# A decoder layer on one Trainium2 core: keys and values in one token-major projection, the keys then turned by two transposes

## The chip, the core and the metric

One core of a Trainium2 chip runs the whole kernel. Its engines work side by side, each in its own order, and wait for each other by semaphores: PE (TensorE, matrix products), DVE (VectorE), ACT (ScalarE), POOL (GpSimd) and SP (SyncE, which here only starts DMAs). PE reads SBUF and writes PSUM, which has eight banks of 512 fp32 columns; DVE and ACT read PSUM. The metric is the device time of one execution in microseconds (us), lower is better.

## The reference

A layer of three parts on x of 8 batches x 256 tokens x 512 features, in fp32: a recurrent mixing block with a gated MLP, a cross-attention, and a mixture of experts. The change lies in the cross-attention:

```
q = (Q @ w_q.T).reshape(B, S, G, HG, HD)      # G=8 groups, HG=4 heads each, HD=16
k = (K @ w_k.T).reshape(B, S, G, HD)          # K = V = ctx, 8 x 256 x 512; w_k is 128 x 512
v = (V @ w_v.T).reshape(B, S, G, HD)          # w_v is 128 x 512
scores = jnp.einsum('bnghd,bmgd->bnghm', q, k) / scale
...
attn = jax.nn.softmax(scores, axis=-1)
out = jnp.einsum('bnghm,bmgd->bnghd', attn, v).reshape(B, S, D)
return out @ w_o.T + b_o
```

Scores are masked causally and by a padding mask. The result is added to x, whose rows were normalised before the projection of the queries.

## The kernel before, in words

**Products in three parts.** A projection in fp32 is made of fp32r matmuls: each operand is split into a rounded part (hi) and a rest (lo), and `three` (L780) issues hi x hi, lo x hi, hi x lo into one PSUM region. The first operand is the stationary one (128 columns at most), the second the moving one, streamed column by column.

**Keys, values, queries of a batch.** `keys` (L906) keeps a block of weights stationary and streams the 256 tokens of the context: 4 feature blocks x 3 = 12 matmuls of 256 columns; the result is k transposed (feature by token), as the scores need it. `values` (L912) keeps 128 tokens of the context stationary and streams 128 weight columns: 2 token tiles x 4 x 3 = 24 matmuls of 128 columns; the result is token by feature. `queries` (L920) makes half of q transposed in 24 matmuls of 256 columns.

**The cross-attention in passes.** After the MLP, eight passes, one for each batch, of 24 steps (`pass_c`; PE's at L1092). The tables at L111 to L114 set the order. `TURNED` puts the two transposes of the normalised rows of the next batch but one step ahead of probabilities (steps 3 and 6). `SUMMED` names the pieces that share PSUM bank 7: before, keys of the next batch at step 3, values at 6, query halves at 11 and 19, output projections at 14 and 22. PE issues such a piece in its step (`summed_piece`, L1078) as soon as DVE has read the piece before it out of the bank (semaphore `sum_read`); DVE reads it in its next step (`summed_read`, L1805), by `keys_read` (L1727), `values_read` (L1734) or `queries_read` (L1740). At the start of every fourth step PE makes the scores of a set of four units (`scores`, L1013, into banks 0 to 3; L1019 and L1022), for which DVE must have finished the maxima of the set before. At each step PE transposes the probabilities of the unit four steps back (L1030) into bank 4 or 5 in turn, which it may write once ACT has copied out (L1422) what stood there two turns ago; the transposes of h (L903) take turns in the same two banks. At steps 5, 9, 13 and so on it sums over the values (`attend`, L1037; L1048 and L1054).

**DVE's order in a pass** (`pass_c` at L1831): in step u first the reading of the piece of step u - 1, then the maxima (`maxes`, L1815; L1829): of units u and u + 1 in the first step of a set, of unit u + 1 in the next two, none in the fourth. Then, at steps 7, 11, 15 and 23, a group of finished heads (`heads_read`, L1782: transpose, reciprocal, scaling, L1786 to L1799), and statistics for later stages.

**Batch 0's pieces** are made before pass 0, inside the last step of the MLP (`first_pieces`): keys and values in front of the last down projection, the queries behind it. DVE's reading counts in semaphore `first`; scores of pass 0 wait for four of them.

**Contexts.** SP loads a batch's context, POOL splits it (`ctx_split`, L636), and may overwrite the split one once the values are made.

Of the kernel before, what the change touches and what calls it, by code (L numbers as in the profile page):

```python
# [110 lines left out]
TURNED = {3: "hT0", 6: "hT1"}  # L111
SUMMED = {3: "kT", 6: "v", 11: "qT0", 14: "wo1", 19: "qT1", 22: "wo0"}

# [85 lines left out]
def decoder_layer(nc: bass.Bass, x, weights, ctx_t, mask, h_rows, out):  # L199
    with ExitStack() as es:  # L200
# [130 lines left out]
        o_div = at("o_div", [P, D], F32)  # L331
        hc = at("hc", [P, TPB, D], F32)
        assert place[0] <= hd_at
        region(raw0_at)
# [35 lines left out]
        def signals(prefix, **meanings):  # L370
# [20 lines left out]
            h="tiles normalised", hT_ps="tiles of h transposed in PSUM", hT_first="the first batch's copied out", hT="tiles of h transposed and split",  # L391
            kT_ps="batches with k^T in PSUM", v_ps="batches with v in PSUM", q_ps="halves of q^T in PSUM", first="the first batch's k, v and q in SBUF",
            o_rawT="tiles of o, feature-major", oT_hi="the last one's hi", oT="tiles of o split", wo_ps="tiles of the output projection in PSUM",
# [116 lines left out]
        def _(pool):  # L510
# [126 lines left out]
            def ctx_split(b):  # L637
                if b == 0:
                    pool.wait_ge(mlp["up"], JB * (CHUNKS * (MLP_GROUPS - 1) + 1))
                pool.wait_ge(c["ctx"], 16 * b + 16)  # L640
                after(pool, c["v_ps"], b)
                chc.link(nc.gpsimd.tensor_copy(ctx_s[:, 0, :, :], ctx_raw[:, :, :]))
                nc.gpsimd.tensor_tensor(out=ctx_s[:, 1, :, :], in0=ctx_raw[:, :, :], in1=ctx_s[:, 0, :, :], op=ALU.subtract).then_inc(c["ctx_s"], 1)
# [176 lines left out]
        def _(pe):  # L820
# [84 lines left out]

            def keys(bank):  # L906
                for kb in range(KB):
                    o = KB * D + kb * 2 * P
                    mm = three(pe, bank[:, 0:SEQ], slot_block(0, 0, o, P), slot_block(0, 1, o, P), ctx_s[:, 0, kb, :], ctx_s[:, 1, kb, :], kb == 0, kb == KB - 1)
                mm.then_inc(c["kT_ps"], 1)  # L910

            def values(bank):  # L912
                for t in range(TPB):
                    n = slice(t * P, (t + 1) * P)
                    for kb in range(KB):
                        o = KB * D + kb * 2 * P + P
                        mm = three(pe, bank[:, n], ctx_s[:, 0, kb, n], ctx_s[:, 1, kb, n], slot_block(0, 0, o, P), slot_block(0, 1, o, P), kb == 0, kb == KB - 1)
                mm.then_inc(c["v_ps"], 1)

# [8 lines left out]
            def first_pieces(qs):  # L928

                if qs:  # L930
                    pe.wait_ge(c["hT"], TPB)
                    for half in range(2):
                        queries(half, ps[:, 2 + half, :])
                    return
                pe.wait_ge(mlp["m"], JB * CHUNKS * MLP_GROUPS)
                for t in range(TPB):
                    turn_h(0, t, ps[:, 2 + t, :])
                pe.wait_ge(w_ready[0], SLOT_X // 2 + 1)
                pe.wait_ge(c["ctx_s"], 1)
                keys(ps[:, 0, :])  # L940
                values(ps[:, 1, :])

# [90 lines left out]
            def attend(b, s):  # L1033
                if s == 0:
                    if b == 0:
                        pe.wait_ge(c["first"], 4)
                    else:  # L1037
                        pe.wait_ge(sum_read, sum_turn("v", b - 1) + 1)
                for u in (4 * s + 2, 4 * s + 3):
                    turned_unit(b, u)  # L1040
                if s != 3 and s != 5:
                    after(pe, c["o_div"], 4 * b + (0, 1, 2, 2, 3)[s])
                pb = b % 2
                if s < FIRST_SETS:
                    for a in range(2):
                        for j in range(4):
                            p_in = pt[:, (4 * s + j) % PLACES, :].rearrange("p (i a t) -> p a i t", a=2, t=P)[:, a]
                            mm = nc.tensor.matmul(ps[32 * j:32 * j + 32, 6, a * SEQ:(a + 1) * SEQ], v32[:, pb, 0, 4 * a + j, :], p_in, start=True, stop=True)  # L1048
                else:
                    for a in range(2):  # L1050
                        o = a * SEQ + (s - FIRST_SETS) % 2 * P
                        for m in range(TPB):
                            for j in range(4):
                                mm = nc.tensor.matmul(ps[32 * j:32 * j + 32, 6, o:o + P], v32[:, pb, m, 4 * a + j, :],  # L1054
                                                      pt[:, (4 * s + j) % PLACES, (2 * a + m) * P:(2 * a + m + 1) * P], start=(m == 0), stop=(m == TPB - 1))
                mm.then_inc(c["O"], 1)
# [21 lines left out]
            def summed_piece(name, b):  # L1078
                after(pe, sum_read, sum_turn(name, b))
                of = b + batch_of(name)  # L1080
                if not 0 <= of < BATCH:
                    pe.sem_inc(sum_read, 1)
                elif name == "kT":
                    pe.wait_ge(c["ctx_s"], of + 1)
                    keys(ps[:, 7, :])
                elif name == "v":
                    values(ps[:, 7, :])
                elif name[0] == "q":
# [36 lines left out]
            for b in range(BATCH):  # L1125
                if b == BATCH - 1:
                    pe.wait_ge(c["v_ps"], BATCH)
                    pe.wait_ge(c["q_ps"], 2 * BATCH)
                    pe.sem_inc(w_free[0], 1)
                pass_c(b)  # L1130
# [114 lines left out]
            up_d(0)  # L1245
            for name in ("kT", "v", "qT0"):
                summed_piece(name, BATCH)
# [344 lines left out]
        def _(dve):  # L1592
# [140 lines left out]

            def values_read(b, bank, signal):  # L1734
                dve.wait_ge(c["v_ps"], b + 1)
                for t in range(TPB):
                    ins = nc.vector.tensor_copy(v32[:, b % 2, t, :, 0:HD], bank[:, t * P:(t + 1) * P].rearrange("p (g d) -> p g d", g=KVG))
                ins.then_inc(signal, 1)
# [18 lines left out]
            def first_pieces():  # L1757
# [5 lines left out]
                dve.wait_ge(c["ones"], 2)  # L1763
                keys_read(0, ps[:, 0, :], c["first"])
                values_read(0, ps[:, 1, :], c["first"])
                h_c(1, 0)
# [9 lines left out]
            with dve.Fori(1, MLP_GROUPS // 2 - 1) as i:  # L1776
                steps(i * (2 * CHUNKS), 2, False)
            steps((MLP_GROUPS // 2 - 1) * 2 * CHUNKS, 2, True, meanwhile={1: first_norm, 2: first_rows, 3: first_pieces})
            for half in range(2):
                queries_read(0, half, ps[:, 2 + half, :], c["first"])  # L1780
# [25 lines left out]
            def summed_read(name, b):  # L1806
                of = b + batch_of(name)
                if not 0 <= of < BATCH:
                    return
                if name == "kT":  # L1810
                    keys_read(of, ps[:, 7, :], sum_read)
                elif name == "v":
                    values_read(of, ps[:, 7, :], sum_read)
                elif name[0] == "q":
# [384 lines left out]
```

## Time and profile before

| | |
|---|---|
| three runs | 1391.21, 1391.97, 1394.29 us |
| median | 1391.97 us |
| profiled execution: span from its first to its last instruction | 1390.5 us |
| profiled execution: its own time around the span | not listed |
| PE busy | 1340.8 us, 96% of the span |
| PE weight loads | 1068.0 us, 77% |
| DVE busy | 819.9 us, 59% |
| ACT busy | 606.6 us, 44% |
| POOL busy | 513.0 us, 37% |

The busy shares are means over stages with different limits. The attention's passes show in the page's slices as the stretch in which DVE rises to 7 and 8 tenths and ACT to 7. Weight loads run beside the matmuls. The ends of matmuls are modelled and overlap the start of the next, so the cost of a group of matmuls is read from the start of its first to the start of what follows it.

### The profile page before, as it was taken

The numbers are of one execution on the slowest core, as the hardware profiler recorded it, in microseconds if no ns is written. First come the engines' busy times: TensorE is split into PE (matmuls) and PEld (weight loads), VectorE is DVE, ScalarE is ACT, GpSimd is POOL, SyncE is SP. The second block draws the span as 40 slices with busy tenths as digits, with TensorE's granted clock in tenths as the row PEclk, the third lists the DMA queues.
The fourth block names the chain that finished last, engine by engine and source line by source line (L and its number), as shares of the span: only waits on it lengthen the run. The fifth ranks groups of instructions, "written<-read, shape, count | busy, mean of one in ns | idle before, by whom it ended". The sixth has DMA issues, their size and how long they took to land.

```text
span 1390.5 us, 23678 instructions
## 1 busy us (share of the span) xinstructions
PE 1340.8 (96%) x8180; PEld 1068.0 (77%) x8180; DVE 819.9 (59%) x2085; ACT 606.6 (44%) x1135; POOL 513.0 (37%) x485
## 2 busy tenths in 40 slices
PE   8999999999999999999999999999988999999994
PEld 6788888888888888888886777777766877766762
DVE  5888865333333333333467787788786586666661
ACT  4444441111111111111126777777786324777772
POOL 4555542202020202020427554446453112655552
PEclk9999999999999999999999999999999999999997
DMA  6000002010110101010100000000011924566553
GB/s 257 1 0 0 0 30 107 0 46 5 42 38 8 45 0 45 0 46 1 49 12 17 21 21 21 21 5 17 6 47 46 374 81 159 92 106 105 95 98 46
DMA packets 20533, 73.41 MB, mean 53 GB/s; under 512 B 2320, under 2 KB 3344, under 8 KB 18000
## 3 DMA queue, kind: packets, MB, share of 16 engines
q1 hardware_dynamic: 10256, 46.93, 9.3%
q0 software_dynamic: 10176, 25.17, 9.2%
q8 instruction: 59, 0.97, 0.3%
q14 instruction: 42, 0.34, 0.1%
HBM read 52.95 MB, written 19.14 MB: 52 GB/s over the span
## 4 chain that ended last, share of the span: by engine, by line
PE 86%; DVE 6%; ACT 4%; issue 2%; DMA 1%; POOL 1%; POOLq 0%; DVEq 0%; SPq 0%; ACTq 0%
PE ps L782 21%; PE ps L784 21%; PE ps L783 21%; PE ps L1030 5%; PE ps L1215 5%; PE ps L1022 2%; DVE den L1641 2%; ACT cols L1434 2%; PE ps L1054 2%; PE ps L1122 2%; PE ps L1048 1%; ACT cols L1422 1%; PE ps L1185 1%; PE ps L1143 1%; PE ps L1019 1%
## 5 line engine op out<-in xcount | busy, mean ns | idle before, releaser
L782 PE MATMUL ps<-feat,wsplit 128*128 128x512 f32 (+1 forms) x672 | 247.1, 368 | 3.2 <-PE ps L784 2.1
L784 PE MATMUL ps<-feat,wsplit 128*128 128x512 f32 (+1 forms) x672 | 244.6, 364 | 0.0
L783 PE MATMUL ps<-feat,wsplit 128*128 128x512 f32 (+1 forms) x672 | 244.5, 364 | 0.0
L1291 ACT ACTIVATE sg<-ps 128x512 f32<-128x512 f32 x64 | 38.3, 598 | 369.1 <-PE ps L784 369.0
L1561 DVE TENSOR_TENSOR m_f<-ps,sg 128x512 f32<-128x512 f32 x64 | 44.2, 691 | 245.4 <-ACT sg L1291 245.4
L542 POOL CAST wsplit<-wraw 128x3072 fp32r<-128x3072 f32 x9 | 24.8, 2755 | 399.3 <-PEq L970 386.7
L1829 DVE CUSTOM_DVE_ANT_0 cols<-ps,msk 128x256 f32<-128x256 f32 (+1 forms) x512 | 146.2, 353 | 27.7 <-PE ps L1022 16.3
L782 PEld LDWEIGHTS ps<-feat,wsplit 128*128 128x128 f32 x672 | 126.7, 189 | 26.4 <-issue 6.6
L1422 ACT COPY cols<-ps 128x512 f32<-128x512 f32 x192 | 111.6, 581 | 77.7 <-PE ps L1030 77.7
L784 PEld LDWEIGHTS ps<-feat,wsplit 128*128 128x128 f32 x672 | 126.6, 188 | 19.9
L783 PEld LDWEIGHTS ps<-feat,wsplit 128*128 128x128 f32 x672 | 126.7, 189 | 19.7
L1030 PEld LDWEIGHTS ps<-ident,cols 128*128 128x128 f32 x768 | 83.5, 140 | 45.0 <-issue 24.0
L1434 ACT ACTIVATE cols<-cols,mxs 128x256 f32<-128x256 f32 x256 | 116.8, 508 | 0.9 <-DVE mxs L1829 0.5
L1030 PE MATMUL ps<-ident,cols 128*128 128x128 f32 x768 | 109.6, 279 | 3.6 <-ACT cols L1422 3.6
L756 POOL DMA_INDIRECT out<-yx,ids x39 | 75.3, 1930 | 83.7 <-DMA out<-yx,ids 52.7
L1569 DVE TENSOR_TENSOR acc<-ps,acc 128x512 f32<-128x512 f32 x128 | 84.9, 686 | 25.5 <-PE ps L784 25.5
L674 POOL TENSOR_TENSOR cols<-mxs,cols 128x512 f32<-128x512 f32 x64 | 64.6, 1042 | 88.9 <-DVE mxs L1829 88.9
L782 PE MATMUL ps<-wsplit,hTa 128*128 128x512 f32 x192 | 77.1, 401 | 2.0 <-DVE hTa L1622 1.4
L784 PE MATMUL ps<-wsplit,hTa 128*128 128x512 f32 x192 | 75.4, 393 | 0.0
L783 PE MATMUL ps<-wsplit,hTa 128*128 128x512 f32 x192 | 75.2, 392 | 0.0
L1215 PE MATMUL ps<-rawx,mT_x 128*128 x156 | 73.4, 592 | 0.6 <-ACT mT_x L1486 0.6
L2033 DVE TENSOR_TENSOR up_even<-rawx,up_even 128x1024 fp32r<-128x1024 f32 x40 | 49.2, 1231 | 26.2 <-ACT up_even L1502 22.9
(281 smaller groups left out, 3014.5 us busy)
## 6 DMA issues: line engine op xcount, KB each, us to landing
wraw<-weights SPq DMA_DIRECT2D x11, 1536.0 KB, 6.5
rawx<-weights SPq DMA_DIRECT2D x8, 1536.0 KB, 16.1
ctx_raw<-ctx_t SPq DMA_DIRECT2D x8, 512.0 KB, 4.6
h_rows<-hd POOLq DMA_DIRECT2D x16, 256.0 KB, 4.4
out<-acc SPq DMA_DIRECT2D x4, 1024.0 KB, 4.7
qkv_raw<-weights SPq DMA_DIRECT2D x6, 512.0 KB, 7.5
acc<-x SPq DMA_DIRECT2D x1, 3072.0 KB, 17.5
acc<-x SPq DMA_DIRECT2D x2, 512.0 KB, 7.0
```

Of the source, the lines that this page charges most:

```text
L674: nc.gpsimd.tensor_tensor(out=s_u, in0=m_u, in1=s_u, op=ALU.subtract).then_inc(c["sub"], 1)
L756: pool.indirect_dma_start(out=out[:, :], out_offset=bass.IndirectOffsetOnAxis(ap=ids[:, s:s + 1], axis=0), in_=yx[:, g % 3, :], in_offset= ...
L782: nc.tensor.matmul(out_, w_hi, m_hi, start=first, stop=False)
L783: nc.tensor.matmul(out_, w_lo, m_hi, start=False, stop=False)
L784: return nc.tensor.matmul(out_, w_hi, m_lo, start=False, stop=last)
L1030: tr = nc.tensor.transpose(ps[:, 4 + k, i * P:(i + 1) * P], sc[:, u % PLACES, i * P:(i + 1) * P], ident[:, :])
L1215: mm = nc.tensor.matmul(ps[:, 4 + g % 2, :], mT_x[:, g % 2, j, :], raw[:, o:o + D], start=(j == 0), stop=(j == JB - 1))
L1422: nc.scalar.copy(pt[:, u % PLACES, :], bank).then_inc(turned[k], 1)
L1434: ins = nc.scalar.activation(part, part, ACT.Exp, bias=mxs[:, u % PLACES, n:n + 1], scale=-1.0)
L1569: nc.vector.tensor_tensor(acc[:, tile, :], ps[:, 4 + t, :], acc[:, tile, :], ALU.add).then_inc(s_["acc"], 1)
L1829: ins = nc.vector.tensor_tensor_reduce(sc[:, at_, n * w:(n + 1) * w], ps[:, u % 4, n * w:(n + 1) * w], m_in, -0.25, 3e38, ALU.add, ALU.min ...
L2033: nc.vector.tensor_tensor(w[:, 1, o], rawx[:, bass.ds(raw[g], 1), o].rearrange("p o n -> p (o n)"), w[:, 0, o], ALU.subtract).then_inc(d[" ...
```

## The change

The weights of keys and values lie next to each other in the slot, 128 columns of keys and 128 of values for each feature block. `keys_values` keeps 128 tokens of the context stationary and streams all 256 columns: 2 x 4 x 3 = 24 matmuls of 256 columns, which make keys and values of a batch token by feature, in bank 7. DVE copies the keys into a new tile `k_tok` in SBUF and the values where they went before. `keys` is now two transposes of `k_tok` into bank 7, which DVE reads with the two instructions that it read the keys with. In the passes the merged piece stands at step 6 and the transposes at step 9; step 3 has no piece. The context is waited for at step 6. For batch 0 the transposes stand behind the MLP's last down projection, ahead of the queries.

```
-SUMMED = {3: "kT", 6: "v", 11: "qT0", 14: "wo1", 19: "qT1", 22: "wo0"}
+SUMMED = {6: "kv", 9: "kT", 11: "qT0", 14: "wo1", 19: "qT1", 22: "wo0"}
...
+        k_tok = at("k_tok", [P, TPB, P], F32)
...
-            def keys(bank):
-                for kb in range(KB):
-                    o = KB * D + kb * 2 * P
-                    mm = three(pe, bank[:, 0:SEQ], slot_block(0, 0, o, P), slot_block(0, 1, o, P), ctx_s[:, 0, kb, :], ctx_s[:, 1, kb, :], kb == 0, kb == KB - 1)
-                mm.then_inc(c["kT_ps"], 1)
-
-            def values(bank):
+            def keys_values(bank):
                 for t in range(TPB):
                     n = slice(t * P, (t + 1) * P)
                     for kb in range(KB):
-                        o = KB * D + kb * 2 * P + P
-                        mm = three(pe, bank[:, n], ctx_s[:, 0, kb, n], ctx_s[:, 1, kb, n], slot_block(0, 0, o, P), slot_block(0, 1, o, P), kb == 0, kb == KB - 1)
-                mm.then_inc(c["v_ps"], 1)
+                        o = KB * D + kb * 2 * P
+                        mm = three(pe, bank[:, t * 2 * P:(t + 1) * 2 * P], ctx_s[:, 0, kb, n], ctx_s[:, 1, kb, n], slot_block(0, 0, o, 2 * P), slot_block(0, 1, o, 2 * P),
+                                   kb == 0, kb == KB - 1)
+                mm.then_inc(c["kv_ps"], 1)
+
+            def keys(bank):
+                for t in range(TPB):
+                    tr = nc.tensor.transpose(bank[:, t * P:(t + 1) * P], k_tok[:, t, :], ident[:, :])
+                tr.then_inc(c["kT_ps"], 1)
...
                 if qs:
+                    pe.wait_ge(c["first"], 1)
+                    keys(ps[:, 1, :])
...
+                elif name == "kv":
+                    pe.wait_ge(c["ctx_s"], of + 1)
+                    keys_values(ps[:, 7, :])
                 elif name == "kT":
-                    pe.wait_ge(c["ctx_s"], of + 1)
                     keys(ps[:, 7, :])
...
-            def values_read(b, bank, signal):
-                dve.wait_ge(c["v_ps"], b + 1)
+            def keys_values_read(b, bank, signal):
+                dve.wait_ge(c["kv_ps"], b + 1)
+                by_token = bank.rearrange("p (t a n) -> p a t n", t=TPB, a=2)
+                nc.vector.tensor_copy(k_tok[:, :, :], by_token[:, 0])
                 for t in range(TPB):
-                    ins = nc.vector.tensor_copy(v32[:, b % 2, t, :, 0:HD], bank[:, t * P:(t + 1) * P].rearrange("p (g d) -> p g d", g=KVG))
+                    ins = nc.vector.tensor_copy(v32[:, b % 2, t, :, 0:HD], by_token[:, 1, t, :].rearrange("p (g d) -> p g d", g=KVG))
                 ins.then_inc(signal, 1)
```

The order of DVE's instructions in pass 1, from step 7 to the reading of the first query half, before. `v_125` is the tile of values, `cols` holds scores, keys and queries, `mxs` the maxima; the rows of the maxima are one group of eight pairs, of which the first stands here.

```order
L1737 COPY v_125<-ps 128x8x16 [waits c_v_ps]
L1786 STREAM_TRANSPOSE ps<-ps 128x512 [waits c_O]
L1790 RECIPROCAL rden<-ps 128x16 [waits c_o_blk]
L1793 TENSOR_TENSOR o_div<-ps,rden 128x16x16 [waits c_rden]
L1799 STREAM_TRANSPOSE o_rawT<-o_div 128x512 [waits c_oT,c_o_div]
L1829 ISA cols,mxs<-ps,msk 128x256 [waits c_S,c_PT_ps]
L1829 ISA mxs 128x1
L1743 COPY cols<-ps 128x2x256 [waits c_q_ps,c_dve]
```

The same place after (lines 4 higher). The group of maxima is now in two parts, three units and one, with the reading of the keys between them:

```order
L1739 COPY k_tok<-ps 128x256 [waits c_kv_ps]
L1741 COPY v_125<-ps 128x8x16 x2
L1790 STREAM_TRANSPOSE ps<-ps 128x512 [waits c_O]
L1833 ISA cols,mxs<-ps,msk 128x256 [waits c_S,c_PT_ps]
L1833 ISA mxs 128x1
L1733 TENSOR_SCALAR cols<-ps,half_of 128x256 [waits c_half,c_kT_ps]
L1733 TENSOR_SCALAR cols<-ps,half_of 128x256
L1833 ISA cols,mxs<-ps,msk 128x256 [waits c_S,c_PT_ps]
L1747 COPY cols<-ps 128x2x256 [waits c_q_ps,c_dve]
```

The copy of the keys stands ahead of that of the values, and the two instructions that read the turned keys have come here from step 4.

PE's order in the same pass, from the third scores (step 8) to the first query half (step 11), before:

```order
L1022 MATMUL ps<-cols 128x512 [waits c_mx]
L1030 MATMUL ps<-ident,cols 128x128 [waits c_P,c_turned0]
L1030 MATMUL ps<-ident,cols 128x128 [waits c_P,c_turned1]
L1048 MATMUL ps<-cols,v_125 32x256 [waits c_turned1,c_o_div,c_turned0,c_sum_read]
L782 MATMUL ps<-feat,wsplit 128x256 [waits c_hT,c_sum_read]
```

And after (lines 1 or 2 higher):

```order
L1024 MATMUL ps<-cols 128x512 [waits c_mx]
L1032 MATMUL ps<-ident,cols 128x128 [waits c_P,c_turned0]
L918 MATMUL ps<-ident,k_tok 128x128 [waits c_sum_read]
L918 MATMUL ps<-ident,k_tok 128x128
L1032 MATMUL ps<-ident,cols 128x128 [waits c_P,c_turned1]
L1050 MATMUL ps<-cols,v_125 32x256 [waits c_turned1,c_o_div,c_turned0,c_sum_read]
L783 MATMUL ps<-feat,wsplit 128x256 [waits c_hT,c_sum_read]
```

The two transposes stand between the probabilities of two steps. The queries' wait on `c_sum_read` is written as before, but the reading it counts up to is now that of the turned keys.

## Rows read from the trace of the kernel before

**Rows 1.** Busy us of PE, PEld, DVE, ACT, POOL, then clock, one stretch.

```profile
820.00:860.00 40.00, 39.71 (x419) 30.93 (x416) 32.87 (x161) 29.56 (x65) 20.53 (x21) 1.00 0.07 19
```

**Rows 2.** Waits of PE, 740 to 1060 us: line, releaser; total us, times, longest.

```profile
PE ps L903 <- ACT cols L1422: 2.0, 7, 0.3
```

**Rows 3.** Timeline of PE, one pass: start, us, engine, line, operation [idle before].

```profile
858.25 0.66 PE L903 MATMUL ps<-ident,hc 128*128 128x128 f32 x4 [0.29 <-ACT cols L1422]
...
858.66 0.36 PE L782 MATMUL ps<-feat,wsplit 128*128 128x256 f32 x1
...
860.18 0.60 PE L1030 MATMUL ps<-ident,cols 128*128 128x128 f32 x4
...
860.71 1.15 PE L1019 MATMUL ps<-cols 32*128 32x256 f32 x16
...
864.23 0.31 PE L782 MATMUL ps<-wsplit,feat 128*128 128x128 f32 x1
...
866.95 1.06 PE L1030 MATMUL ps<-ident,cols 128*128 128x128 f32 x8
...
867.94 1.14 PE L1022 MATMUL ps<-cols 32*128 32x512 f32 x8
...
871.44 0.36 PE L782 MATMUL ps<-feat,wsplit 128*128 128x256 f32 x1
...
874.40 0.60 PE L1030 MATMUL ps<-ident,cols 128*128 128x128 f32 x4
```

**Rows 4.** Timeline of DVE in the same pass.

```profile
859.16 0.08 DVE L1829 DVE_READ_ACCUMULATOR2_ANT mxs<- 128x1 f32 x1
...
860.38 0.88 DVE L1731 TENSOR_SCALAR cols<-ps,half_of 128x256 f32<-128x256 f32 x2 [0.32 <-PE ps L784]
...
867.15 0.49 DVE L1737 COPY v<-ps 128x128 f32<-128x128 f32 x2 [0.67 <-PE ps L784]
...
869.70 0.39 DVE L1829 CUSTOM_DVE_ANT_0 cols<-ps,msk 128x256 f32<-128x256 f32 x1
...
872.43 0.73 DVE L1786 STREAM_TRANSPOSE ps<-ps 128x512 f32<-128x512 f32 x1
```

**Rows 5.** Timeline of ACT in the same pass.

```profile
857.62 0.58 ACT L1422 COPY cols<-ps 128x512 f32<-128x512 f32 x1
...
858.62 0.59 ACT L1422 COPY cols<-ps 128x512 f32<-128x512 f32 x1
```

**Rows 6.** DVE groups by line and shape, 740 to 1060 us (busy, mean ns).

```profile
L1743 DVE COPY cols<-ps 128x512 f32<-128x512 f32 x14 | 9.7, 690 | 3.4 <-PE ps L784 2.7
...
L1737 DVE COPY v<-ps 128x128 f32<-128x128 f32 x14 | 3.4, 286 | 5.4 <-PE ps L784 5.4
```

**Rows 7.** Timeline of PE, batch 0's pieces and pass 0.

```profile
716.23 0.36 PE L782 MATMUL ps<-feat,wsplit 128*128 128x256 f32 x1
...
720.37 0.44 PE L782 MATMUL ps<-wsplit,m_odd 128*128 128x512 f32 x1
...
738.25 1.15 PE L1019 MATMUL ps<-cols 32*128 32x256 f32 x16 [2.10 <-DVE mxs L1829]
...
744.78 1.14 PE L1022 MATMUL ps<-cols 32*128 32x512 f32 x8
...
748.28 0.36 PE L782 MATMUL ps<-feat,wsplit 128*128 128x256 f32 x1
```

**Rows 8.** Timeline of DVE in pass 0.

```profile
746.25 0.42 DVE L1829 CUSTOM_DVE_ANT_0 cols<-ps,msk 128x256 f32<-128x256 f32 x1 [1.77 <-PE ps L1022]
```

**Rows 9.** Two stretches as in rows 1, and PE in the second.

```profile
732.00:742.00 10.00, 6.88 (x70) 5.53 (x70) 7.33 (x58) 3.86 (x7) 6.18 (x7) 1.00 0.01 2
...
1064.00:1070.00 6.00, 5.42 (x48) 4.06 (x49) 4.95 (x10) 2.46 (x4) 1.62 (x3) 0.72 0.24 87
...
1064.58 1.43 PE L1122 MATMUL ps<-ident,hd 128*128 128x128 f32 x8 [1.20 <-DVE hT_first L1880]
```

More of the change, by code:

```diff
@@ L391, in decoder_layer @@
             h="tiles normalised", hT_ps="tiles of h transposed in PSUM", hT_first="the first batch's copied out", hT="tiles of h transposed and split",
-            kT_ps="batches with k^T in PSUM", v_ps="batches with v in PSUM", q_ps="halves of q^T in PSUM", first="the first batch's k, v and q in SBUF",
+            kT_ps="batches with k^T in PSUM", kv_ps="batches with k and v in PSUM, token-major", q_ps="halves of q^T in PSUM", first="the first batch's k, v and q in SBUF",
             o_rawT="tiles of o, feature-major", oT_hi="the last one's hi", oT="tiles of o split", wo_ps="tiles of the output projection in PSUM",
@@ L640, in ctx_split @@
                 pool.wait_ge(c["ctx"], 16 * b + 16)
-                after(pool, c["v_ps"], b)
+                after(pool, c["kv_ps"], b)
                 chc.link(nc.gpsimd.tensor_copy(ctx_s[:, 0, :, :], ctx_raw[:, :, :]))
@@ L939, in first_pieces @@
                 pe.wait_ge(c["ctx_s"], 1)
-                keys(ps[:, 0, :])
-                values(ps[:, 1, :])
+                keys_values(ps[:, 0, :])
             def run_mlp(s_):
@@ L1037, in attend @@
                     else:
-                        pe.wait_ge(sum_read, sum_turn("v", b - 1) + 1)
+                        pe.wait_ge(sum_read, sum_turn("kv", b - 1) + 1)
                 for u in (4 * s + 2, 4 * s + 3):
@@ L1082, in summed_piece @@
                     pe.sem_inc(sum_read, 1)
+                elif name == "kv":
+                    pe.wait_ge(c["ctx_s"], of + 1)
+                    keys_values(ps[:, 7, :])
                 elif name == "kT":
-                    pe.wait_ge(c["ctx_s"], of + 1)
                     keys(ps[:, 7, :])
-                elif name == "v":
-                    values(ps[:, 7, :])
                 elif name[0] == "q":
@@ L1126, in _ @@
                 if b == BATCH - 1:
-                    pe.wait_ge(c["v_ps"], BATCH)
+                    pe.wait_ge(c["kv_ps"], BATCH)
                     pe.wait_ge(c["q_ps"], 2 * BATCH)
@@ L1245, in _ @@
             up_d(0)
-            for name in ("kT", "v", "qT0"):
+            for name in ("kv", "kT", "qT0"):
                 summed_piece(name, BATCH)
@@ L1763, in first_pieces @@
                 dve.wait_ge(c["ones"], 2)
-                keys_read(0, ps[:, 0, :], c["first"])
-                values_read(0, ps[:, 1, :], c["first"])
+                keys_values_read(0, ps[:, 0, :], c["first"])
                 h_c(1, 0)
@@ L1778, in _ @@
             steps((MLP_GROUPS // 2 - 1) * 2 * CHUNKS, 2, True, meanwhile={1: first_norm, 2: first_rows, 3: first_pieces})
+            keys_read(0, ps[:, 1, :], c["first"])
             for half in range(2):
@@ L1809, in summed_read @@
                     return
-                if name == "kT":
+                if name == "kv":
+                    keys_values_read(of, ps[:, 7, :], sum_read)
+                elif name == "kT":
                     keys_read(of, ps[:, 7, :], sum_read)
-                elif name == "v":
-                    values_read(of, ps[:, 7, :], sum_read)
                 elif name[0] == "q":
```

## The prediction

> **What bounds the kernel now.** I read the stretches first, then PE's waits, then one pass of the cross-attention instruction by instruction on PE and DVE. The edit touches the eight passes from 733 to 1060 us and the end of the MLP before them. There PE is the bound: in a 40 us stretch it is busy 39.71 us, DVE 32.87, ACT 29.56, POOL 20.53 [rows 1]. PE hardly waits: the most regular wait is 0.29 us once a pass, in front of the first turned tile of h, for ACT's copy, seven times 2.0 us in all [rows 2]. So less PE work in a pass shortens it, unless PE then meets an engine that was early until now. DVE is the candidate: 82% busy, and read in one fixed order.
>
> **One pass, as it is (passes 1 to 6 repeat it).** PE: the turned h at 858.25, keys from 858.66 to 860.18 (1.52 us, 12 matmuls of 256 columns), probabilities, second scores, values from 864.23 to 866.95 (2.72 us, 24 of 128 columns), third scores at 867.94, first queries from 871.44 to 874.40 (2.96 us, 24 of 256 columns) [rows 3]. So one matmul costs 0.113 us with 128 columns and 0.123 with 256: a column is nearly free up to 256, and that is what the change uses. DVE: it reads the keys at 860.38 (0.88 us) after 0.32 us of idling, so this read costs nothing today; it reads the values at 867.15 after 0.67 us of idling, then does one group of heads, starts the third set's maxima at 869.70 and has done four units at 872.43 (2.73 us) [rows 4].
>
> The Trainium skill, "TensorE: Matmul & The Clock Gate", section "Back-to-back issue gap", gives 134 cycles for 128 columns and 262 for 256, an estimate of 56 and 109 ns at 2.4 GHz: by it merging saves PE nothing. This trace has 113 and 123 ns, so the sum goes by the trace; what the rule would give is the last rival.
>
> **The change, part by part, in a pass from 1 to 6.**
> - *Keys leave step 3 (PE).* 1.52 us go. What is late next is the same step's transposes: they write the PSUM bank that the transposes of step 2 filled, and ACT copies that out from 858.62 for 0.59 us, to 859.21 [rows 5]. ACT to PE takes 0.05 us (857.62 + 0.58 = 858.20 against 858.25) [rows 3, 5]. So step 3's transposes start at 859.26 instead of 860.18: 0.92 us gained of 1.52. If that wait were not there, the next bound is DVE, which finishes the first set's maxima at 859.24 (859.16 + 0.08 [rows 4]): the second scores, now at 859.26 + 0.53 = 859.79, could start at 859.29, 0.50 better, no more.
> - *Keys and values at step 6 (PE).* 24 matmuls of 256 columns for 24 of 128: 2.96 for 2.72, +0.24 us [rows 3]. Third scores: 859.26 + (867.94 - 860.18) + 0.24 = 867.26, so PE is 0.68 us ahead of before.
> - *The copy of the keys (DVE).* 128x256 from PSUM to SBUF, an operation the trace lacks. Nearest: 0.286 us for 128 columns and 0.690 for 512 [rows 6]; between them 0.42, less the 0.08 by which neighbours overlap (two of 0.286 took 0.49 [rows 4, 6]): 0.34. Ends: 0.20 (as 128 columns) and 0.61 (as 512). It stands ahead of the copies of the values, on the path that follows.
> - *The keys' read moves from step 4 to step 10 (DVE).* Same two instructions, 0.88 us, but now behind the third set's first three units and ahead of its fourth. And the queries at step 11 wait until DVE has read the previous piece out of their shared bank. Before, that was the values, read long ago; now it is the turned keys. DVE's chain: PE's step 6 piece gives way to the next at 859.26 + (866.95 - 860.18) + 0.24 = 866.27, DVE starts reading 0.20 later, as today, at 866.47; + 0.34 copy; + 2.55 copies of the values and heads (867.15 to 869.70); + 2.05 three of four units of 2.73; + 0.88 keys' read = 872.29; + 0.05 to PE = 872.34 [rows 4].
> - *Two transposes (PE), step 9.* Four take 0.41 us [rows 3], so two 0.21. They wait for DVE's reading of keys and values, over at 867.3; PE comes there past 868, so no wait. Without the new wait the queries would start at 867.26 + (871.44 - 867.94) + 0.21 = 870.97.
> - *Sum.* Queries at 872.34 instead of 871.44: PE stands 1.37 us, eats the 0.47 it was ahead, and the pass is **0.90 us longer**. Everything behind the queries waits for PE or was early, so it shifts as a whole; six passes, +5.40.
>
> **Pass 0.** There keys cost PE nothing: it waits 2.10 us behind them until 738.25 for DVE's first maxima [rows 7]. No heads are read either. The third scores come at 744.78 + 0.24 = 745.02 [rows 7]; DVE, which starts their maxima at 746.25 [rows 8], starts at 746.49; + 2.05 + 0.88 + 0.05 = 749.47 for the queries against 748.28: **+1.19**.
>
> **Batch 0's pieces in the end of the MLP.** Keys and values take 716.23 to 720.37, 4.14 us [rows 7]; 24 matmuls of 256 take 2.96, and two transposes 0.21 more: **-0.97**. The transposes wait for DVE's copy, but the whole last down projection lies between; the keys' read (0.88) hides behind 48 query matmuls (5.9 us).
>
> **The clock.** With the keys gone from pass 0, PE idles for the 2.10 us and the keys' 1.5 on top, some 3.5, until the second scores [rows 7]. After the 2.10 the granted clock stayed 1.00 (2.4 GHz); at 1064 us, behind an idle time of 1.20 us, it shows 0.72, a part at 1.2 GHz [rows 9]. So I expect a fall here. Price: that stretch lost 0.28 of its 6 us of clock, 1.68. Behind the idle time PE has the second scores, transposes and the merged piece, but also 0.2 to 0.3 of waiting for ACT as in rows 2; so part of the loss is hidden, I take **1.2**, nearer to the row than to nothing, and keep 0 and 1.7 as ends.
>
> POOL's split of the contexts waits for the merged piece, at the same step as before and ahead of a long idle time; SP's loads follow it. Pass 7 has no next batch and only shifts.
>
> **Total.** 5.40 + 1.19 - 0.97 + 1.2 = +6.8 us. On the profiled span, 1390.5, that is 1397.3. The time of that execution is not listed apart from its span; the three runs are 1391.21, 1391.97 and 1394.29, the median 1.47 above the span, so I forecast 1398.8.
>
> **Rivals.**
> - *The clock stays up* (for it: one idle time alone, with none near; against: it is the longest in the passes). 1.2 less: 1397.6.
> - *The wait is shorter.* If step 3 need not wait for ACT and DVE alone bounds it, each of six passes is 0.50 better: +3.8, 1395.8; with the clock up as well +2.6, 1394.6. For it: ACT's turn comes earlier if its exponentials before it do; against: ACT stands right in front of that copy with another one from 857.62, so it has no time to give [rows 5].
> - *PE's saving arrives (not slower).* One mechanism: DVE reaches the keys' read so early that the queries start when PE is ready, at 870.97, 0.47 earlier a pass. It decides when DVE's chain of 5.82 us from 866.47 comes out at 4.45 or less. Pass 0 then loses 745.02 + 3.50 + 0.21 - 748.28 = 0.45. Sum: 6 x -0.47 + 0.45 - 0.97 + 1.2 = -2.1, 1389.8; without the clock's fall -3.3, 1388.6. For it: DVE has 18% idle time; against: none of it lies inside this chain, all of whose parts are rows.
> - *The copy costs as 512 columns.* It lies on the path in passes 1 to 6 (in pass 0 DVE waits for the third scores anyway): 6 x 0.27 = 1.6 more, 1400.4; at the 128-column end 0.8 less, 1398.0.
> - *Narrow matmuls are cheap.* If 128 columns cost half of 256, 24 of them would be 1.48 us; the merged piece with its 2.96 would cost PE 1.48 more than the values, not 0.24, so 1.24 more in each of seven passes, and batch 0's would save nothing, 1.18 more: 9.9 on top, near 1409. The 0.113 and 0.123 us speak against it. By the table of the Trainium skill's "TensorE: Matmul & The Clock Gate" it would be so; the trace does not agree.
>
> **How the numbers follow.** Forecast 54%; clock stays up 19%; shorter wait 14%; saving arrives 6%; dearer copy 6%; cheap narrow matmuls 1%. About 0.2%, 2.8 us, is what can be told from no change. Slower: 54 + 19 + 6 + 1 and 8 of the 14 for the shorter wait, 88%. The same: its other 6 and 2 of the 6 where the saving arrives, 8%. Faster: the other 4%. Range: from 1394.6, the shorter wait with the clock up, to 1401.0, the dearer copy with the clock's fall at 1.7 us and rounded up; the forecast's own range is 1396.5 to 1400.
>
> **What would show it.** In the profile after: PE waits for DVE's read of the keys (128x256, two instructions) in front of the first queries in passes 0 to 6, 0.7 us in pass 0, near 1.4 in the others, some 9 us in all, where before it had no such wait; 24 merged matmuls take 2.9 to 3.0 us; step 3's transposes wait some 0.5 us for ACT; DVE no longer idles ahead of a keys' read; the clock dips once near 738 us. The first scores of a pass lie 0.9 us further behind those of the pass before. I am wrong if the queries start with no wait for DVE, if the chain from the end of the merged piece to the keys' read is under 5 us, or if the copy is far from 0.42 us.

## The result

The changed kernel takes 1396.06 us (median of 5 runs, 1394.70 to 1397.99), the kernel before 1391.97: a ratio of 1.0033, interval 1.0022 to 1.0044, so it is slower by 3.1 to 6.1 us. The forecast was 1398.8 us, slower. Side and cause came out as forecast; its terms for the clock and for the end of the kernel were wrong and that for pass 0 was too large, and all three made it too high.

The profiled execution of the changed kernel took 1396.96 us, its span is 1395.2 us. The waits of PE from 700 to 1080 us (line, releaser; us in total, times, longest):

```profile
PE ps L783 <- DVE cols L1733: 7.2, 7, 1.1
PE ps L1032 <- ACT cols L1424: 6.0, 13, 1.3
...
PE ps L904 <- ACT cols L1424: 1.7, 6, 0.3
```

In the kernel before, the second of them was:

```profile
PE ps L1030 <- ACT cols L1422: 3.6, 7, 1.3
```

The first line is new: once in each of passes 0 to 6 the queries (L783) wait for DVE's read of the turned keys (L1733). In the second, six waits are new: step 3's transposes now wait for ACT, as forecast. The last is the wait of [rows 2], 2.0 us in 7 there. One pass on PE, to be laid beside [rows 3] (start, us, engine, line, operation, idle time before):

```profile
857.53 1.15 PE L1021 MATMUL ps<-cols 32*128 32x256 f32 x16
...
861.68 0.66 PE L904 MATMUL ps<-ident,hc 128*128 128x128 f32 x4 [0.29 <-ACT cols L1424]
862.74 0.63 PE L1032 MATMUL ps<-ident,cols 128*128 128x128 f32 x4 [0.40 <-ACT cols L1424]
863.29 1.15 PE L1021 MATMUL ps<-cols 32*128 32x256 f32 x16
...
866.82 0.36 PE L783 MATMUL ps<-wsplit,feat 128*128 128x256 f32 x1
...
869.77 1.03 PE L1032 MATMUL ps<-ident,cols 128*128 128x128 f32 x8
870.74 1.14 PE L1024 MATMUL ps<-cols 32*128 32x512 f32 x8
...
872.30 0.38 PE L918 MATMUL ps<-ident,k_tok 128*128 128x128 f32 x2
...
874.05 0.66 PE L1032 MATMUL ps<-ident,cols 128*128 128x128 f32 x4
875.82 0.39 PE L783 MATMUL ps<-feat,wsplit 128*128 128x256 f32 x1 [1.11 <-DVE cols L1733]
```

The four transposes at 874.05 stood in the kernel before at:

```profile
871.03 0.66 PE L1030 MATMUL ps<-ident,cols 128*128 128x128 f32 x4
```

There the queries followed 0.41 us after their start (871.44 in [rows 3]; the printed lengths of matmul groups overlap by 0.25); here it is 1.77. So the wait costs 1.36 us, 0.25 more than the idle time printed beside it. The same pass on DVE, beside [rows 4]:

```profile
869.97 0.43 DVE L1739 COPY k_tok<-ps 128x256 f32<-128x256 f32 x1 [0.92 <-PE ps L785]
870.31 0.48 DVE L1741 COPY v<-ps 128x128 f32<-128x128 f32 x2
...
872.85 0.39 DVE L1833 CUSTOM_DVE_ANT_0 cols<-ps,msk 128x256 f32<-128x256 f32 x1
...
874.89 0.87 DVE L1733 TENSOR_SCALAR cols<-ps,half_of 128x256 f32<-128x256 f32 x2
```

From 869.97 on the view prints no idle time of DVE: copy, values, heads, three units, the keys' read, and right behind its end (875.76) PE starts. Pass 0 and batch 0's pieces, beside [rows 7]:

```profile
716.92 0.36 PE L783 MATMUL ps<-wsplit,feat 128*128 128x256 f32 x1
...
719.88 0.40 PE L783 MATMUL ps<-wsplit,m_odd 128*128 128x512 f32 x1
...
737.49 1.15 PE L1021 MATMUL ps<-cols 32*128 32x256 f32 x16 [3.16 <-DVE mxs L1833]
...
745.43 1.14 PE L1024 MATMUL ps<-cols 32*128 32x512 f32 x8
...
749.90 0.39 PE L783 MATMUL ps<-feat,wsplit 128*128 128x256 f32 x1 [0.50 <-DVE cols L1733]
```

Batch 0's piece takes 2.96 us; the idle time in pass 0 has grown from 2.10 to 3.16 us. The clock behind it (columns as in [rows 1]; the clock is the last but two):

```profile
736.00:738.00 2.00, 0.51 (x8) 0.50 (x12) 1.44 (x14) 1.58 (x3) 2.00 (x4) 1.00 0.00 0
738.00:740.00 2.00, 2.00 (x20) 1.51 (x15) 1.14 (x11) 1.25 (x4) 1.92 (x4) 0.73 0.04 8
740.00:742.00 2.00, 2.00 (x11) 1.93 (x10) 2.00 (x19) 1.06 (x4) 2.00 (x3) 0.50 0.00 0
742.00:744.00 2.00, 2.00 (x18) 2.00 (x17) 0.32 (x4) 1.07 (x2) 2.00 (x3) 0.92 0.01 4
```

Where [rows 9] had 1.00 from 732 to 742, the clock is at 0.50, the 1.2 GHz level, once.

From first scores to first scores, passes 1 to 6 take 42.73 us, from 857.53 above to

```profile
900.27 0.50 PE L1021 MATMUL ps<-cols 32*128 32x256 f32 x4
```

for 41.81 before:

```profile
854.11 0.50 PE L1019 MATMUL ps<-cols 32*128 32x256 f32 x4
...
895.91 0.50 PE L1019 MATMUL ps<-cols 32*128 32x256 f32 x4
```

That is +0.92 each, and in none of these twelve passes does the clock fall, so the clock isn't what lengthens them.

### The profile page after: what moved, and what is told of

The parts are those of the page before. It is cut to its first block, busy times and chain, and to the rows that moved or that the text cites. A ratio compares the mean times of both kernels' runs of the same rounds, so it can differ in the third digit from the quotient of the medians.

```text
span 1395.2 us, 23527 instructions
## 1 busy us (share of the span) xinstructions
PE 1336.4 (96%) x8100; PEld 1062.5 (76%) x8100; DVE 819.5 (59%) x2093; ACT 605.8 (43%) x1135; POOL 516.3 (37%) x485
## 4 chain that ended last, share of the span: by engine, by line
PE 82%; DVE 8%; ACT 4%; issue 3%; DMA 1%; POOL 1%; DVEq 0%; POOLq 0%; ACTq 0%
PE ps L783 21%; PE ps L785 21%; PE ps L784 21%; PE ps L1217 5%; PE ps L1032 4%; ACT cols L1436 2%; PE ps L1024 2%; DVE den L1643 2%; PE ps L1056 2%; PE ps L1124 2%; ACT cols L1424 1%; DVE cols L1833 1%; PE ps L1145 1%; PE ps L1187 1%; PE ps L1021 1%
## 5 line engine op out<-in xcount | busy, mean ns | idle before, releaser
L783 PE MATMUL ps<-feat,wsplit 128*128 128x512 f32 (+1 forms) x640 | 237.6, 371 | 10.2 <-DVE cols L1733 7.2
L785 PE MATMUL ps<-feat,wsplit 128*128 128x512 f32 (+1 forms) x640 | 235.4, 368 | 0.0
L784 PE MATMUL ps<-feat,wsplit 128*128 128x512 f32 (+1 forms) x640 | 235.4, 368 | 0.0
L783 PEld LDWEIGHTS ps<-feat,wsplit 128*128 128x128 f32 x640 | 120.5, 188 | 34.5 <-DVE cols L1733 8.8
L785 PEld LDWEIGHTS ps<-feat,wsplit 128*128 128x128 f32 x640 | 120.5, 188 | 20.0
L784 PEld LDWEIGHTS ps<-feat,wsplit 128*128 128x128 f32 x640 | 120.6, 188 | 19.7
L757 POOL DMA_INDIRECT out<-yx,ids x39 | 79.0, 2025 | 79.4 <-DMA out<-yx,ids 48.0
L783 PE MATMUL ps<-wsplit,hTa 128*128 128x512 f32 x192 | 77.2, 402 | 1.9 <-DVE hTa L1624 1.4
```

Of the source, the lines that this page charges most:

```text
L757: pool.indirect_dma_start(out=out[:, :], out_offset=bass.IndirectOffsetOnAxis(ap=ids[:, s:s + 1], axis=0), in_=yx[:, g % 3, :], in_offset= ...
L783: nc.tensor.matmul(out_, w_hi, m_hi, start=first, stop=False)
L784: nc.tensor.matmul(out_, w_lo, m_hi, start=False, stop=False)
L785: return nc.tensor.matmul(out_, w_hi, m_lo, start=False, stop=last)
```

## The experiments

The theory: the new place of the keys' read on DVE, right ahead of a piece of PE that wants its bank, lengthens the passes, not the merged product. The rivals: DVE is the bound wherever the read stands; the merged product itself is dear; the clock is the loss. "First scores" are the ones that open a pass. Each kernel was timed against the kernel before, whose medians were 1390.65 to 1392.16 us in these comparisons.

### e4: the order without the merging

```
-SUMMED = {3: "kT", 6: "v", 11: "qT0", 14: "wo1", 19: "qT1", 22: "wo0"}
+SUMMED = {6: "v", 9: "kT", 11: "qT0", 14: "wo1", 19: "qT1", 22: "wo0"}
...
```

The pieces themselves are those of the kernel before; the rest of the edit (...) moves the waits for the contexts.

> The kernel before, with its own two pieces (12 matmuls of 256 columns for the keys, 24 of 128 for the values), but the values at step 6 and the keys at step 9. The order alone, nothing merged. Theory 1: step 3 gives only 0.9 of its 1.52 us back because its transposes then wait for ACT, and the keys cost 1.52 at step 9, so passes 1 to 6 take about 42.4 us; DVE's keys' read is over 0.3 us before PE comes to the queries, so the wait there is about nothing; pass 0 about 39.0 to 39.8, with the clock falling near 738 us; in all about 1397 to 1398. Theory 2: nothing new is done, so the time of before, 1392.

Measured: 1396.24 us, ratio 1.0037 (1.0023 to 1.0050). Passes 1 to 6 take 42.39 us, 0.58 more than before, with no wait in front of the queries. PE's new wait is in this row (3.6 us in 7 waits before):

```profile
PE ps L1031 <- ACT cols L1424: 6.0, 13, 1.3
```

Taking 1.52 us of keys out of step 3 brings the second scores only 0.85 us forward, since the transposes there then wait 0.39 us for ACT and lose the overlap with the keys; behind the third scores the same keys cost 1.43 again. So the order alone loses 0.6 us a pass: the place given up was partly free. The total is no clean reading of that: in the profiled execution, the slowest of the five, pass 0 took 41.0 us, with a longer stretch at half clock.

### e3: the keys' copy twice

```
...
+                    nc.vector.tensor_copy(k_two[:, :, :], ps[:, 7, :].rearrange("p (t a n) -> p a t n", t=TPB, a=2)[:, 0])
                     keys_values_read(of, ps[:, 7, :], sum_read)
```

The tile `k_two` is read by nobody.

> The changed kernel, in whose passes DVE copies the keys of the merged piece twice, the first time into a tile that nobody reads. Theory 1 (the copy lies on the path from the merged piece to the keys' read): passes 1 to 6 take 0.34 us more, 43.07, the wait in front of the queries 1.45; pass 0 as it is, since DVE waits there for the third scores anyway; 2.0 us more in all, 1398.1. Theory 2 for this part (DVE has idle time, the copy is hidden): 42.73 and 1396.1.

Measured: 1399.32 us, ratio 1.0062 (1.0046 to 1.0079). Passes 1 to 6 take 43.06 us, 0.33 more than the changed kernel; the second copy starts 0.34 us behind the first:

```profile
869.04 0.42 DVE L1817 COPY k_two<-ps 128x256 f32<-128x256 f32 x1 [0.91 <-PE ps L786]
869.38 0.41 DVE L1740 COPY k_tok<-ps 128x256 f32<-128x256 f32 x1
```

What DVE does ahead of the keys' read reaches the end of the pass one to one: it lies on the path. The total, 1.2 us above the 1398.1 expected, isn't explained by this profile: the profiled execution took 1396.53 us at a mean granted clock of 0.994, the other three 1399.15 to 1400.02 at 0.989 to 0.992.

### e2: the transposes one step later

```
-SUMMED = {6: "kv", 9: "kT", 11: "qT0", 14: "wo1", 19: "qT1", 22: "wo0"}
+SUMMED = {6: "kv", 10: "kT", 11: "qT0", 14: "wo1", 19: "qT1", 22: "wo0"}
```

> The changed kernel with the transposes at step 10 instead of 9; DVE then reads the turned keys one unit of maxima later. Theory 1 (DVE's chain sets the start of the queries): each of passes 0 to 6 takes 0.68 us more, 43.4 for passes 1 to 6, the wait in front of the queries grows from 1.1 to 1.8; 1396.1 + 4.8 = about 1401. Theory 2 (the wait is a side effect, the work is the cost): 42.7 and 1396 as they are.

Measured: 1407.31 us, ratio 1.0121 (1.0106 to 1.0137). Passes without a clock fall take 43.43 us, 0.70 more than the changed kernel, which is one unit of DVE (0.68) and as forecast. The other 6 us were in no theory:

```profile
880.09 0.39 PE L783 MATMUL ps<-feat,wsplit 128*128 128x256 f32 x1 [1.80 <-DVE cols L1733]
```

```profile
880.00:882.00 2.00, 1.91 (x10) 1.91 (x11) 1.93 (x5) 0.00 (x0) 1.99 (x2) 0.58 0.00 0
882.00:884.00 2.00, 2.00 (x12) 2.00 (x12) 0.20 (x2) 0.00 (x0) 1.93 (x1) 0.56 0.00 0
```

Behind the wait of 1.80 us (the first row) the clock (the last column but two of the others) fell in passes 3, 5 and 6, and these take 44.90 to 44.93, 1.48 more each: 4.4 us. Pass 0, with a longer stretch at half clock, took 41.41, 1.93 more than in the changed kernel instead of 0.68. In the changed kernel, with 1.11 us, the clock fell behind none of these waits.

### e1 and e8: the merged piece in step 3

e1 puts the merged piece where the keys were and the transposes where the values were; DVE copies the keys out in step 4 and, in step 7, reads the turned keys and the values.

```
-SUMMED = {6: "kv", 9: "kT", 11: "qT0", 14: "wo1", 19: "qT1", 22: "wo0"}
+SUMMED = {3: "kv", 6: "kT", 11: "qT0", 14: "wo1", 19: "qT1", 22: "wo0"}
...
```

> The merged piece stands at step 3 and the transposes at step 6; DVE copies only the keys in step 4, and reads the turned keys and copies the values in step 7. The transposes write into the keys' own columns, so the values stay in the bank meanwhile. Theory 1 (the changed kernel is longer because the keys' read stands late in DVE's order and the queries wait for it): the wait of PE in front of the first queries goes, passes 1 to 6 take about 41.0 us (41.81 before, 42.73 changed), pass 0 about 35.9 (37.50 before), the clock does not fall near 738 us, in all about 1385 us. Theory 2 (the new work itself, 256 columns, the copy, the transposes, costs more than it saves, wherever it stands): passes stay above 41.8 and the time above 1392.

Measured: 1392.53 us, ratio 1.0011 (1.0002 to 1.0020): about 3 us better than the changed kernel, but not the gain expected, and by the numbers alone what the second theory gave. Passes 1 to 6 take 41.8 to 42.8 us where 41.0 were expected, and pass 0 takes 38.37 where 35.9 were: PE waits 1.59 us for ACT there (to 743.72) and the clock falls right behind it. PE's wait in front of the queries is gone, and another is there (the first row; below it DVE in step 7 of a pass):

```profile
PE ps L1050 <- DVE o_div L1797: 5.9, 6, 1.3
```

```profile
869.59 0.88 DVE L1821 TENSOR_SCALAR cols<-ps,half_of 128x256 f32<-128x256 f32 x2
870.38 0.48 DVE L1823 COPY v<-ps 128x128 f32<-128x128 f32 x2
870.78 0.72 DVE L1790 STREAM_TRANSPOSE ps<-ps 128x512 f32<-128x512 f32 x1
...
871.83 0.42 DVE L1797 TENSOR_TENSOR o_div<-ps,rden 128x256 f32<-128x256 f32 x1
```

The summation (L1050) waits until the heads have been divided out of its bank, and the two reads, 1.19 us, now stand ahead of the heads. e8 turns these two round and nothing else:

```
-                    if u - 1 in SUMMED:
+                    if u - 1 in SUMMED and u != 7:
...
+                    if u == 7:
+                        summed_read(SUMMED[6], b)
```

The added lines stand behind `heads_read`.

> The kernel of e1 (merged piece in step 3, transposes in step 6), with one more edit: in step 7 DVE reads the heads first and the turned keys and the values only behind them. In the trace of e1, PE waits 1.0 to 1.35 us for DVE's division of the heads in front of the transposes of the output in passes 2 to 6, and 0.3 in pass 1. Theory (these two copies stand on a path that ends at PE, as the copy and the keys' read do in the changed kernel, and only their place is wrong): these waits go, passes 1 to 6 take 41.4 us (42.4 in e1, 41.8 in the kernel before), and the kernel takes about 1387.5 us, 4 less than the kernel before. Rival (DVE, which works there without a break, is itself the bound): the wait comes back in front of the next scores or queries, the passes stay at 42.3, and the time at 1392.

Measured: 1388.05 us, ratio 0.9973 (0.9962 to 0.9984). Passes 1 to 6 take 41.4 to 42.0 us, 41.67 in the mean (41.4 expected), with 0.2 us of that wait left, once. The rival, DVE as the bound (42.3 us a pass, 1392 in all), fails here.

### e9: queries first, then the transposes

```
-SUMMED = {6: "kv", 9: "kT", 11: "qT0", 14: "wo1", 19: "qT1", 22: "wo0"}
+SUMMED = {6: "kv", 9: "qT0", 11: "kT", 14: "wo1", 19: "qT1", 22: "wo0"}
```

> The changed kernel with two pieces exchanged: the first queries in step 9, the transposes of the keys in step 11, so that no piece of PE stands right behind the keys' read of DVE. Theory (the chain that ends with the keys' read is what lengthens the pass): the wait of 1.11 us in front of the queries goes and no other comes, since PE does 2.96 us of queries and two steps more before it wants the bank again; passes 1 to 6 take 41.6 us (42.73 in the changed kernel), pass 0 0.5 us less, and the time is about 1389 us. Rival (DVE is the bound of the pass, wherever the read stands): the wait moves to the transposes of the keys or to the output, the passes stay at 42.5 or more and the time at 1395 to 1396.

Measured: 1387.43 us, ratio 0.9968 (0.9956 to 0.9981), the lowest median of all, though its interval overlaps that of e8. The same merged product, the same DVE work, two pieces exchanged. PE in a pass:

```profile
855.23 0.50 PE L1021 MATMUL ps<-cols 32*128 32x256 f32 x4
...
869.91 0.36 PE L783 MATMUL ps<-feat,wsplit 128*128 128x256 f32 x1
...
874.89 0.38 PE L918 MATMUL ps<-ident,k_tok 128*128 128x128 f32 x2
...
896.60 0.50 PE L1021 MATMUL ps<-cols 32*128 32x256 f32 x4
```

Neither queries nor transposes wait; the pass is 41.37 us. That is 1.36 less than in the changed kernel, the whole cost of the wait (more than the 1.11 that had been counted on), and 0.44 less than before, where the forecast's third rival gave 0.47 if the wait were not there. The merged product is a gain; its order made it a loss. Only pass 0 missed: it took 40.17 us where 0.5 less than the changed kernel's 39.5 was expected, with a longer stretch at half clock.

### e5 and e10: work in the idle time of pass 0

e5 is the changed kernel with 12 unused matmuls of 256 columns in step 3 of pass 0; e10 is the kernel before with 18 of 128 columns there.

> The changed kernel with 12 matmuls of 256 columns at step 3 of pass 0 alone, whose result nobody reads. They fill the 3.2 us in which PE idles there. If the idle time is what makes the clock fall near 739 us, it does not fall, and pass 0 takes about 38.7 us instead of 39.48, the rest as it is: some 0.8 us less in all. If the fall is chance, it comes in some runs with the filler too and pass 0 stays at 39.5.

Measured: 1394.79 us, ratio 1.0027 (1.0016 to 1.0038); the interval overlaps that of the changed kernel, so the time doesn't settle it. In the profile PE waits 1.7 us there, the clock stays at 1.00 (one stretch of it below), and pass 0 takes 38.29 us. One profile doesn't settle it either: in e3 the clock stayed up behind 3.2 us of waiting, without added work.

```profile
740.00:742.00 2.00, 2.00 (x19) 2.00 (x18) 2.00 (x19) 0.87 (x3) 2.00 (x3) 1.00 0.00 0
```

> The kernel before, with 18 matmuls of 128 columns more in step 3 of pass 0, whose result nobody reads: PE idles 2.1 us right behind them, so they cost the pass nothing (18 by 0.113 us is 2.0). In the profiles of all three kernels with the old pieces an instruction load (one packet of 16 KB, about 1.2 us) starts 38.7 us behind the first scores of pass 7, 0.4 us ahead of the stores of rows of h; the first store then lands 3.5 to 3.9 us behind its issue, and PE waits 0.8 to 1.2 us in front of the first turned rows of h. In all eight with the merged piece the loads lie elsewhere, the stores land in 2.6 us and this wait is missing. Theory (where the load falls follows from the number of PE's instructions ahead of it, and a load on top of the stores delays them): 18 matmuls with their 18 weight loads bring that load 1 to 2 us earlier, to 36.5 to 37.8, the stores land in 2.6 us, the wait is gone, and from the first scores of pass 7 to the end it takes about 346 to 346.5 us in place of 347.1 or more; the kernel takes about 1390, 1.2 less than before. Rival (the stores are slow in the kernel before for another reason): the stores still take 3.5 us or more, the wait of about 1 us stays, and the time is that of the kernel before, 1391.2.

Measured: 1390.23 us, ratio 0.9985 (0.9976 to 0.9994), a little better than before. Pass 0 takes 37.46 us at full clock. From the first scores of pass 7 to PE's last instruction it takes 348.32 us where 346 to 346.5 were expected: the clock falls 144.8 us behind these scores, as it does in the first profile of the changed kernel (144.0, 347.78 us in all). What the filler does ahead of that fall is in the next section.

### e6 and e7: both kernels profiled once more

> The kernel before, once more with its profile. From the first scores of pass 7 to the last PE instruction the profile before took 349.5 us, the changed one 347.2. If what differs there (how long a store of rows takes to land near 1063 us, 3.5 against 2.0 us of DVE waiting, and a fall of the clock behind it) is chance, this run shows some value from 347 to 350 and its waits another landing. If the change itself gives 2.3 us back there, this run shows 349.5 again.

> The changed kernel, once more with its profile. Passes 1 to 6 again 42.73 us, pass 0 near 39.5 with the clock falling near 739 us if that is what the idle time does, 38.7 if the fall was chance. From the first scores of pass 7 to the last PE instruction anything from 347 to 350 if that stretch varies by itself, 347.2 if the change gives it back.

Measured: 1391.24 and 1395.11 us. This pair is the better one to compare: in both the clock fell once in pass 0 and not again before the kernel's last 15 us. In the kernel before, one stretch of pass 0:

```profile
740.00:742.00 2.00, 2.00 (x15) 1.43 (x8) 1.16 (x11) 0.69 (x2) 1.92 (x3) 0.50 0.00 0
```

So the fall that was forecast for the changed kernel happens to the kernel before as well. Its price is 1.17 us there (pass 0: 38.67 against 37.50 us in the first profile) and 1.18 in the changed order (39.50 against 38.32 in e3, where the clock stayed up behind an idle time of 3.2 us).

The second find is behind the passes. From the first scores of pass 7 to PE's last instruction it is 347.13 us before and 346.08 after, and the difference begins at one wait. (In the first two profiles it is 350.06 and 347.78, each with a fall of the clock in this stretch.) Before, PE's wait and DVE's:

```profile
PE ps L1122 <- DVE hT_first L1880: 0.9, 1, 0.9
```

```profile
DVE hd L1875 <- DMA h_rows<-hd: 3.2, 1, 3.2
```

And its DMAs from 1060 to 1068 us (a queue's packets, MB and share; an issue's count, KB and median us to landing):

```profile
q8 instruction: 1, 0.02, 0.9%
h_rows<-hd POOLq DMA_DIRECT2D x4, 256.0 KB, 3.7
```

In the changed kernel, DVE's wait and the same stores from 1064.7 to 1072.7 us, with no packet of q8 beside them:

```profile
DVE hd L1879 <- DMA h_rows<-hd: 2.0, 1, 2.0
```

```profile
h_rows<-hd POOLq DMA_DIRECT2D x4, 256.0 KB, 2.6
```

DVE overwrites a buffer of h that POOL's DMA has stored, and waits for that store. Before, one packet of instructions (16 KB, 1.17 us) starts 0.4 us ahead of the stores' first packets, and they land in 3.7 us instead of 2.6. All three profiles of kernels with the old pieces have that packet 38.7 us behind the first scores of pass 7 and PE's wait of 0.8 to 1.2 us; in all eight with the merged piece the packets lie elsewhere (32 to 34 and 44 to 45 us), the stores land in 2.5 to 2.6 us and PE doesn't wait. Up to PE's next long wait, for oT, it is 52.9 to 53.0 us behind the first scores of pass 7 in all eight, and 54.1 in e6; what follows varies by itself (e3, with the merged piece and no fall of the clock, takes 347.32 in all). A merged piece with its transposes has 10 matmuls and 10 weight loads fewer than the two pieces, and the theory is that the packets therefore come at other moments. e10 moved the packet by adding instructions to the kernel before (PE's wait, and the DMAs from 1059 to 1067 us):

```profile
PE ps L1128 <- DVE hT_first L1886: 0.3, 1, 0.3
```

```profile
q8 instruction: 1, 0.02, 0.7%
h_rows<-hd POOLq DMA_DIRECT2D x4, 256.0 KB, 3.0
```

The packet came only 0.36 us earlier (38.37; 1 to 2 had been expected), and ended sooner; already the stores land in 3.0 us, 0.3 us of PE's wait is left, and the wait for oT comes at 53.5. In all four kernels with the old pieces the first store lands 1.6 to 1.8 us behind the packet's end (40.05, 39.91, 39.77 and 39.29 us behind the first scores of pass 7). Other stores show the same. One of the later stores of these rows, 2.3 us in all other profiles, took 3.30 in e10 and 2.79 in e4, each with a packet beside it, and an earlier one took 2.69 in the changed kernel (e7), where a packet ended later than in the other seven. So a store beside a packet lands late in either kernel; that the number of PE's instructions sets where it falls is borne out in direction only.

## Why the prediction was right, and where it was not

| term | forecast, us | measured, e6 to e7, us |
|---|---|---|
| ahead of batch 0's pieces (start of turning h: 716.41 to 715.85) | 0 | -0.56 |
| batch 0's pieces (start of turning h to first scores: 17.55 to 16.46) | -0.97 | -1.09 |
| pass 0 (38.67 to 39.50) | +1.19 | +0.83 |
| passes 1 to 6 (250.74 to 256.36 together) | +5.40 | +5.62 |
| the clock's fall | +1.2 | 0 |
| behind the first scores of pass 7 (347.13 to 346.08) | 0 | -1.05 |
| sum | +6.8 | +3.8 |

The sum is that of the two spans (1389.5 to 1393.3); the medians of the result differ by 4.1. The first row is no part of the change: the kernels don't differ there, and the start of turning h lay at 715.43 and 716.41 us in the two profiles of the kernel before.

- *Keys out of step 3.* Right. The transposes wait for ACT, and the second scores, 6.61 us behind the first before, are 5.76 behind them: 0.85 gained, 0.92 forecast. Third scores: 0.63, forecast 0.68.
- *The merged piece.* Right: 2.95 us (866.82 to 869.77) for 2.96. In e4 the 24 values of 128 columns take 2.71, 0.113 each. By the table of isolated matmuls in the Trainium skill, "TensorE: Matmul & The Clock Gate", section "Back-to-back issue gap", an estimate of 56 against 109 ns, the merged piece would have cost about twice the values; the trace doesn't agree, and e9's shorter pass speaks against it a second time. The prediction took that table for the page's rule: the section itself says that the isolated gap under-counts narrow matmuls that each load weights, with about 81 ns for 128 columns, which lies nearer to the 113 ns here.
- *The copy.* Right: 0.34 us of the path by the rows, 0.33 by doubling it.
- *The chain of DVE.* Right: 5.79 us (869.97 to 875.76) for 5.82; the wait costs 1.36 us for 1.37. The "saving arrives" rival fell because that chain had to be 4.45 or less; e9 shows that the saving was there (0.44 us a pass of its 0.47) and that the order kept it from arriving.
- *Pass 0.* The sign and the wait were right (0.50 us in front of the queries, 0.7 forecast), the size 0.36 us too large. The sum kept the second scores in their place, 5.26 us behind the first; they came 4.89 behind them, as DVE began its maxima 1.37 us behind the first scores (733.97, 732.60) instead of 1.74 (734.73, 732.99). Why it began sooner stays open.
- *The clock.* This step failed, though its price was right (1.2 forecast, 1.17 and 1.18 measured). The fall was charged to the change because the one profile of before didn't show it. It comes in both kernels, in some executions: without work added in pass 0, the profiles show it there in the kernel before once of two, in the changed kernel both times, and in the four other orders with 3.2 to 3.5 us of waiting there (e2, e3, e4, e9) three times, then for longer. So the longer wait may make it likelier. How often it comes over all runs isn't known, and a net part of it for the change stays open.
- *The tail.* "Pass 7 has no next batch and only shifts" was wrong by 1.05 us. The waits of PE, the row of L1122 with 1.20 us of idle time ahead of it among them [rows 9], were read as fixed; this one hung on a store that met an instruction load.

## What to carry to other kernels

Count an operation's place as well as its length: the same merged product lost 0.92 us a pass or won 0.44, by whether the read that frees a shared bank stands right ahead of the piece that wants it. Where two pieces share a bank, put the one whose result is read late in an engine's order ahead of a long stretch of other work. And take the profile of before twice before charging a clock fall or a store's wait to a change.

## What was not expected of the hardware

An instruction load shows in the trace as a DMA packet beside the kernel's own: 16 KB, 0.9 to 1.4 us, and 256 KB stores issued beside one landed in 3.5 to 3.9 us (three profiles) instead of 2.5 to 2.6 (eight). And the printed idle time of PE understates a wait: the 1.11 us in front of the queries cost 1.36, as 0.25 us by which the printed lengths of matmul groups overlap is lost as well.
